# Two scan inputs in one GpSimd instruction, in a fused state-space scan and mixture-of-experts kernel

## The chip, the core and the metric

The kernel runs on one core of a Trainium2 chip. The metric is the device time of one execution in microseconds, lower is better. The core's engines work in parallel, each through its own queue in order, and wait for one another through semaphores. In the profile's names PE is TensorE, DVE is VectorE, ACT is ScalarE, POOL is GpSimd and SP is SyncE, which here issues all transfers.

## The reference, cut to what matters

The input is x of 4 x 1024 tokens by 512 channels. Each batch row passes a modulated layer norm, a depthwise convolution over time that gives `u`, and a selective scan with 16 states per channel:

```python
delta = softplus(einsum('blr,dr->bld', dt, dtproj_w) + dtproj_b)
deltaA = exp(delta[..., None] * A)                       # A: 512 x 16
deltaBu = delta[..., None] * Bm[:, :, None, :] * u[..., None]
h = dA * h + dBu                                         # one step in time
y = einsum('bdn,bn->bd', h, c)
```

Then `x = x + ga * (y + u * D_skip)`, a second modulated norm, and a layer of 8 experts, of which the best two are weighted per token: an up projection to 2048, silu, and a down projection to 512. Weights are float32.

## The kernel before, in words

**Tiles.** The 4096 tokens are 8 chunks of `CT` = 512. In a chunk the scan runs over channel tiles of 128 channels (`r`, 4 of them) and states (`n`, 16 of them), so a chunk has 64 *slots*, numbered `slot(c, n, r)`: r runs fastest. A slot is four steps on four engines:

- ACT, task `da` (line 1065): exp(DEL * AN) into one of two PSUM banks, `DA`.
- POOL, task `dbu` (line 837): `DB = DU * BR`, 128x512, where `DU` is delta*u of the channel tile and `BR` is the row of B of state n, spread over the 128 partitions by a DMA (line 644) into one of two buffers. `DB` has `NDB` = 4 slots.
- DVE, task `scan` (line 1297): the recurrence over 512 tokens, from `DA` and `DB` into `H`. From the second chunk of a batch row on it starts from the stored state `ST`, so its form in the profile is `H<-pb,ST,DB` in odd chunks (counted from 0) and `H<-pb,DB` in even ones.
- PE, task `flip` (line 1563), six slots later: four transposes of H into a work bank; then DVE, task `acc` (line 1322), adds C times that bank to `ACC`.

The last chunk (7) is `SPLIT`: its tokens go in two halves, and `dbu` and `scan` have forms of their own (lines 840 and 1302).

**Beside the scans** of a chunk run the attention preparation of the next chunk and the experts of the chunk before (two halves `cs` of 256 tokens). On POOL these are: `cva` (line 784), part of the convolution; `del` and `du` (lines 795, 801), which make DEL and DU of the next chunk late in this one; `g` (line 860), the product that the down projection takes; `sel1` and `sel2` (lines 557 to 569), the expert weights; `hl` (line 808) and `fin` (line 865). DVE has the `conv` taps (line 1256, with two SBUF inputs and a per-partition weight) and `ys` (line 1371), the factor of g that comes from the up projection. ACT has `th` (line 1167), the tanh, which may overwrite a buffer that g of two blocks before has read, and `ud` (line 1052), which waits for `du`. PE has `up` (lines 1612 to 1614) and `dn` (line 1642).

**The order** is one hand-tuned list of tasks (`schedule`, from tables of places in half slots such as `ATTENTION`, `PAIRS` and `ROUTER`), and every engine runs its own tasks of that list in that order. At slot s the list holds scan s, the flip of slot s - 6, da of slot s + 1, dbu of slot s + 2, then the tasks placed at 2s, the accumulations of the flips of slot s - 1, and the tasks placed at 2s + 1. Every fourth slot it holds the DMA of the row of B two states on; that one waits until the dbu of the state two before it are done. The wait of dbu i for its DB slot is for scan i - 4:

```python
                    if i >= NDB:
                        eng.wait_ge(S["scan"], i - NDB + 1)
```

A semaphore that counts scans is at i - 3 when scans 0 to i - 4 are done.

Of the kernel before, what the change touches and what calls it, by code (L numbers as in the profile page):

```python
# [6 lines left out]
CT, FT = 512, 256  # L7
# [4 lines left out]
NDA, NDB, NG = 2, 4, 3  # L12
# [310 lines left out]
def adaln_kernel(nc, x, pvec, alog, ct, wmod, xpT, dtT, wg1T, wg2T, wupT, bup, wdT, bdn, out):  # L323
# [4 lines left out]
    with ctx:  # L328
# [113 lines left out]
        S = {}  # L442
# [271 lines left out]
        def _(eng):  # L714
            for task in order:
# [32 lines left out]
                elif what == "bdz":  # L748
                    eng.wait_ge(S["modp"], rows_done(2))
                    eng.memset(BDX, 0.0).then_inc(S["bdz"], 1)  # L750
                elif what == "gbk":
                    gate, sign = GBC[:, 0], GBC[:, 1]
                    eng.wait_ge(S["gbm"], 1)
                    eng.tensor_scalar(sign, gate, 0.0, 2.0, ALU.is_ge, ALU.mult).then_inc(S["gbclamp"], 1)
                    eng.wait_ge(S["gbclamp"], 1)
                    eng.tensor_scalar(sign, sign, -1.0, 1.0, ALU.add, ALU.mult).then_inc(S["gbclamp"], 1)
                    eng.wait_ge(S["gbclamp"], 2)
                    eng.tensor_tensor(gate, gate, sign, ALU.mult).then_inc(S["gbclamp"], 1)
                    eng.wait_ge(S["gbclamp"], 3)
                    eng.tensor_scalar(gate, gate, 0.25, 1.0, ALU.max, ALU.mult).then_inc(S["gbclamp"], 1)  # L760
                    eng.wait_ge(S["gbclamp"], 4)
                    eng.tensor_tensor(gate, gate, sign, ALU.mult).then_inc(S["gbclamp"], 1)
                elif what == "nma":
                    eng.wait_ge(S["asm"], 4 * k[0])
                    eng.tensor_scalar(ANG[:], ASM[:], -1.0 / D, 1.0, ALU.mult, ALU.mult).then_inc(S["ang"], 1)
                elif what == "nmf":
                    eng.wait_ge(S["fsm"], 2 * (k[0] + 1))
                    eng.tensor_scalar(FNG[:], FSM[:], -1.0 / D, 1.0, ALU.mult, ALU.mult).then_inc(S["fng"], 1)
                elif what == "pad":
                    c = k[0]  # L770
                    if c == 1:
                        eng.wait_ge(S["modp"], rows_done(4))
                    if c >= 2:
                        eng.wait_ge(S["da"], slot(c - 2, NS - 1, 3) + 1)
                    if c % 2:
                        eng.wait_ge(S["hc"], c // 2 + 1)
                        eng.tensor_copy(hm_of(c)[:, :, 0:3], HC[:]).then_inc(S["pad"], 1)
                    else:
                        eng.memset(hm_of(c)[:, :, 0:3], 0.0).then_inc(S["pad"], 1)
                elif what == "cva":  # L780
                    c, dt, tap = k
                    tap_done(eng, c, dt, tap + 1)
                    eng.wait_ge(S["cvs"], nth["cvs", c, dt, tap])
                    eng.tensor_tensor(U[:, dt], U[:, dt], xn_of(c)[:, 2 + nth[task] % 2], ALU.add).then_inc(S["cva"], 1)
                elif what == "hc" and k[0] % 2 == 0:
                    c = k[0]
                    eng.wait_ge(S["hm"], nth["hm", c, 3])
                    if c > 1:
                        eng.wait_ge(S["pad"], c)
                    eng.tensor_copy(HC[:], hm_of(c)[:, :, 512:515]).then_inc(S["hc"], 1)  # L790
                elif what == "del" and k[0]:
                    c, dt = k
                    eng.wait_ge(S["m"], nth["m", c, dt])
                    eng.wait_ge(S["ln"], 4 * c + dt + 1)
                    eng.tensor_tensor(DEL[:, c % 2, dt], DEL[:, c % 2, dt], xn_of(c)[:, dt], ALU.add).then_inc(
                        S["del"], 1)
                elif what == "du" and k[0]:
                    c, dt = k
                    eng.wait_ge(S["ug"], nth["ug", c, dt])
                    eng.wait_ge(S["del"], nth["del", c, dt])  # L800
                    eng.tensor_tensor(DU[:, c % 2, dt], DEL[:, c % 2, dt], U[:, dt], ALU.mult).then_inc(S["du"], 1)
                elif what == "hl":
                    cs, i = k
                    d = slice(2 * i, 2 * i + 2)
                    if cs >= 2:
                        eng.wait_ge(S["up"], (cs - 1) * NM)
                    eng.wait_ge(S["hh"], cs + 1)
                    eng.tensor_tensor(HLV[cs % 2][:, d], H2F[:, d], HHV[cs % 2][:, d].bitcast(f32),
                                      ALU.subtract).then_inc(S["hl"], 1)
                elif what == "wlo":  # L810
                    i, half = k
                    kk, h = divmod(i, 2)
                    sl = slice(h * 1024 + half * 512, h * 1024 + half * 512 + 512)
                    eng.wait_ge(S["whi"], i + 1)
                    taps = [nth[t] for t in order[:at[task]] if t[0] == "conv"]
                    if taps and taps[-1] > 12:
                        eng.wait_ge(S["conv"], taps[-1])
                    eng.tensor_tensor(WUL[:, kk, sl], WS[h][:, half * 512:half * 512 + 512], WUH[:, kk, sl].bitcast(f32),
                                      ALU.subtract).then_inc(S["wlo"], 1)
                elif what == "r4":  # L820
                    cs = k[0]
                    eng.wait_ge(S["rt"], 6 * cs + 4)
                    eng.tensor_copy(IXF[:], IX[:]).then_inc(S["ixf"], 1)
                elif what in ("sel1", "sel2") and k[0] < NF - 2:
                    select(eng, what, k[0])
                elif what == "dbu":
                    c, n, r = k
                    i = slot(c, n, r)
                    _, h, qs, _, _ = part(c, n, r)
                    if n == 0:  # L830
                        eng.wait_ge(S["du"], nth["du", c, qs[-1]])
                    if r == 0:
                        eng.wait_ge(S[f"d_br{n % 2}"], rows_of_b(c, n))
                    if i >= NDB:
                        eng.wait_ge(S["scan"], i - NDB + 1)
                    if h is None:
                        eng.tensor_tensor(DB[:, i % NDB], DU[:, c % 2, r], BR[:, n % 2], ALU.mult).then_inc(S["dbu"], 1)  # L837
                    else:
                        b = BR[:, n % 2, r // 2 * FT:r // 2 * FT + FT]
                        eng.tensor_tensor(DB[:, i % NDB].rearrange("p (k t) -> p k t", k=2),  # L840
                                          DU[:, c % 2, qs[0]:qs[0] + 2, h * FT:h * FT + FT],
                                          b.unsqueeze(1).to_broadcast([128, 2, FT]), ALU.mult).then_inc(S["dbu"], 1)
                elif what == "frs":
                    cs = k[0]
                    eng.wait_ge(S["fsq"], 2 * (cs + 1))
                    eng.tensor_scalar(FRS[:, :, 0], FSQ[:], 1.0 / D, EPS, ALU.mult, ALU.add).then_inc(S["frs"], 1)
                    eng.wait_ge(S["frs"], 3 * cs + 1)
                    eng.tensor_tensor(FRS[:, :, 0], FRS[:, :, 0], MH[:, 0:2], ALU.pow).then_inc(S["frs"], 1)
                    eng.wait_ge(S["frs"], 3 * cs + 2)
                    eng.tensor_tensor(FNM[:, :, 0], FNG[:], FRS[:, :, 0], ALU.mult).then_inc(S["frs"], 1)  # L850
                elif what == "g":
                    cs, m = k
                    i = cs * NM + m
                    eng.wait_ge(S["ys"], i + 1)
                    eng.wait_ge(S["t1"], i + 1)
                    if i >= NG and in_parts((i - NG) // 2):
                        eng.wait_ge(S["gl"], nth["gl", *divmod(i - NG, NM)])
                    elif i >= NG:
                        eng.wait_ge(S["dn1"], i - NG + 1)
                    eng.tensor_tensor(G[:, i % NG], TH[:, m % 2], YS[:, m % 2], ALU.mult).then_inc(S["g"], 1)  # L860
                elif what == "fin":
                    cs, j = k
                    acc = acc_tile(cs // 2, 2 * (cs % 2) + j)
                    eng.wait_ge(S["to"], nth["to", cs, j])
                    eng.tensor_tensor(acc, acc, TO[:, j], ALU.add).then_inc(S["fin"], 1)
# [818 lines left out]
```

## Time and profile before

| what | value |
|---|---|
| three runs | 1390.89, 1391.97, 1392.40 us |
| median | 1391.97 us |
| the profiled execution, first to last instruction | 1389.7 us |
| PE busy | 1310.4 us (94%) |
| DVE busy | 1228.5 us (88%) |
| POOL busy | 1136.4 us (82%) |
| ACT busy | 988.3 us (71%) |
| TensorE clock granted, mean | 0.977 of full speed |

The profile gives the profiled execution's span, 1389.7 us; its own device time is not given apart, and the span lies 2.3 us under the median of the runs. In a row of instructions, `L837 POOL TENSOR_TENSOR DB<-DU,BR ... x448 | 576.6, 1304 | 43.6 <-DVE H L1297 36.7` reads: line 837, on POOL, 448 of them, busy 576.6 us together, 1304 ns each on the mean; POOL was idle for 43.6 us just before them, and of that 36.7 us ended with a scan of line 1297.

### The profile page before, as it was taken

The page shows a single profiled execution, that of the slowest core. Times are in us where ns is not written, and L with a number is a line of the kernel's source. Part 1 is how long each engine was busy: PE and PEld are TensorE (multiplying, and loading weights), DVE is VectorE, ACT ScalarE, POOL GpSimd, SP SyncE. Part 2 cuts the span into 40 slices and gives each one's busy share as a digit, 9 for nine tenths or more (in the row PEclk, how much of TensorE's full clock was granted, in tenths as well). Part 3 has the DMA queues.
Part 4 walks back from the last instruction along what each step waited for, and adds up shares of the span by engine and source line. Part 5 has one row for each costly group of instructions (what it writes and reads, how often), then busy time and mean ns, then how long its engine had stood idle before and what let it go on. Part 6 is the DMA issues. An engine that isn't in the chain of part 4 may idle for free. (4 is left out here: it accounts for less than half of the span.)

```text
span 1389.7 us, 23827 instructions
## 1 busy us (share of the span) xinstructions
PE 1310.4 (94%) x7664; PEld 977.8 (70%) x7664; DVE 1228.5 (88%) x1729; ACT 988.3 (71%) x2110; POOL 1136.4 (82%) x1177
## 2 busy tenths in 40 slices
PE   8888768999999999999999999999999999989998
PEld 4466546767776777777776777767776776768897
DVE  4899999989998999989998999999998999885565
ACT  4875786588857786588858786688758775745654
POOL 1799889799997999799998999799988987762332
PEclk9999867999999999999999999999999999999999
DMA  5542112325342424434342434334253423323342
GB/s 201 177 154 62 61 39 90 115 78 170 94 148 86 161 97 123 132 111 156 90 144 85 164 97 125 125 113 146 87 148 100 129 85 116 108 74 125 112 125 79
DMA packets 99284, 160.94 MB, mean 116 GB/s; under 512 B 9276, under 2 KB 33980, under 8 KB 99160
## 3 DMA queue, kind: packets, MB, share of 16 engines
q1 hardware_dynamic: 99160, 159.42, 36.3%
q8 instruction: 61, 1.00, 0.3%
q14 instruction: 63, 0.52, 0.1%
HBM read 150.60 MB, written 8.79 MB: 115 GB/s over the span
## 5 line engine op out<-in xcount | busy, mean ns | idle before, releaser
L837 POOL TENSOR_TENSOR DB<-DU,BR 128x512 f32<-128x512 f32 x448 | 576.6, 1304 | 43.6 <-DVE H L1297 36.7
L1322 DVE SCALAR_TENSOR_TENSOR ACC<-pb,CTM,ACC 128x512 f32<-128x512 f32 x512 | 373.6, 730 | 42.4 <-PE pb L1563 41.5
L1642 PE MATMUL pb<-WD,G 128*128 128x512 f32 x856 | 406.0, 594 | 0.0
L1065 ACT ACTIVATE pb<-DELP,AN 128x512 f32<-128x512 f32 x448 | 305.8, 685 | 107.5 <-DVE H L1297 105.3
L1563 PE MATMUL pb<-ID,H 128*128 128x128 f32 x2048 | 311.9, 280 | 32.9 <-DVE ACC L1322 25.3
L1563 PEld LDWEIGHTS pb<-ID,H 128*128 128x128 f32 x2048 | 244.0, 144 | 137.0 <-issue 77.5
L1612 PE MATMUL pb<-H2H,WUH 128*128 128x256 f32 x1024 | 326.7, 319 | 12.0 <-DVE TY L1371 11.8
L1297 DVE TENSOR_TENSOR_SCAN H<-pb,DB 128x512 f32<-128x512 f32 x256 | 309.7, 1211 | 13.4 <-ACT pb L1065 12.3
L1614 PE MATMUL pb<-H2H,WUL 128*128 128x256 f32 x1024 | 290.5, 284 | 0.0
L1613 PE MATMUL pb<-H2L,WUH 128*128 128x256 f32 x1024 | 290.2, 283 | 0.0
L860 POOL TENSOR_TENSOR G<-TY 128x256 f32<-128x256 f32 x256 | 188.9, 756 | 99.7 <-ACT TY L1172 44.3
L1297 DVE TENSOR_TENSOR_SCAN H<-pb,ST,DB 128x512 f32<-128x512 f32 x192 | 244.1, 1271 | 7.3 <-ACT pb L1065 7.3
L1642 PEld LDWEIGHTS pb<-WD,G 128*128 128x128 f32 x856 | 149.3, 191 | 108.7 <-issue 107.5
L1612 PEld LDWEIGHTS pb<-H2H,WUH 128*128 128x128 f32 x1024 | 196.3, 192 | 36.2 <-issue 26.4
L1167 ACT ACTIVATE TY<-pb,BUPH 128x256 f32<-128x256 f32 x256 | 108.8, 469 | 149.5 <-PE pb L1614 137.2
L1613 PEld LDWEIGHTS pb<-H2L,WUH 128*128 128x128 f32 x1024 | 196.9, 192 | 13.3 <-issue 12.7
L1614 PEld LDWEIGHTS pb<-H2H,WUL 128*128 128x128 f32 x1024 | 196.2, 192 | 0.0
L1371 DVE SCALAR_TENSOR_TENSOR TY<-pb,BUP,SR 128x256 f32<-128x256 f32 x256 | 110.5, 472 | 35.7 <-ACT TY L1167 32.8
L1172 ACT ACTIVATE TY<-TY 128x256 f32<-128x256 f32 x256 | 102.1, 412 | 0.0
L1302 DVE TENSOR_TENSOR_SCAN H<-pb,ST,DB 128x256 f32<-128x256 f32 x128 | 88.4, 732 | 6.4 <-ACT pb L1070 4.3
L840 POOL TENSOR_TENSOR DB<-DU,BR 128x512 f32<-128x512 f32 x64 | 81.2, 1281 | 4.1 <-DVE H L1302 4.1
L1256 DVE SCALAR_TENSOR_TENSOR U<-DELP,PV,U 128x512 f32<-128x512 f32 x57 | 59.6, 1059 | 0.8
(220 smaller groups left out, 1700.0 us busy)
## 6 DMA issues: line engine op xcount, KB each, us to landing
WD<-in_wdT SPq DMA_DIRECT2D x128, 512.0 KB, 4.7
BR<-bscr SPq DMA_DIRECT2D x112, 256.0 KB, 3.7
SR<-sscr SPq DMA_DIRECT2D x128, 128.0 KB, 4.6
ACC<-in_x SPq DMA_DIRECT2D x16, 512.0 KB, 4.0
out<-ACC SPq DMA_DIRECT2D x32, 256.0 KB, 3.0
DU<-in_x SPq DMA_DIRECT2D x7, 1024.0 KB, 5.6
BR<-bscr SPq DMA_DIRECT2D x32, 128.0 KB, 3.1
DU<-in_xpT SPq DMA_DIRECT2D x7, 320.0 KB, 3.1
```

Of the source, the lines that this page charges most:

```text
L837: eng.tensor_tensor(DB[:, i % NDB], DU[:, c % 2, r], BR[:, n % 2], ALU.mult).then_inc(S["dbu"], 1)
L860: eng.tensor_tensor(G[:, i % NG], TH[:, m % 2], YS[:, m % 2], ALU.mult).then_inc(S["g"], 1)
L1065: eng.activation(DA[i % NDA][:], DEL[:, c % 2, r], ACT.Exp, scale=AN[:, r, n:n + 1]).then_inc(S["da"], 1)
L1167: eng.activation(TH[:, m % 2], up_of(cs, m), ACT.Tanh, scale=0.5, bias=BUPH[:, m:m + 1]).then_inc(S["th"], 1)
L1297: eng.tensor_tensor_scan(H[:, (c * NS + n) % NH, r], DA[i % NDA][:], DB[:, i % NDB], ST[:, n, r:r + 1] if state_from(c, h) else 0.0, ALU.mult,
L1322: eng.scalar_tensor_tensor(out=acc, in0=banks[bank_of["flip", c, n, r]][:], scalar=1.0 if n < 0 else CTM[:, c % 2, j, st:st + 1], in1=acc, ...
L1371: eng.scalar_tensor_tensor(out=YS[:, m % 2], in0=up_of(cs, m), scalar=BUP[:, m:m + 1], in1=SR[:, m // 2 % 2], op0=ALU.add, op1=ALU.mult).t ...
L1563: t = eng.transpose(b[:, dt * 128:dt * 128 + 128], src[:, dt, r * 128:r * 128 + 128], ID[:])
L1612: eng.matmul(b, WUH[:, kk, sl], H2H[:, cs % 2, kk], start=kk == 0, stop=False)
L1613: eng.matmul(b, WUH[:, kk, sl], H2L[:, cs % 2, kk], start=False, stop=False)
L1614: t = eng.matmul(b, WUL[:, kk, sl], H2H[:, cs % 2, kk], start=False, stop=kk == 3)
L1642: eng.matmul(DN[j][:], G[:, (cs * NM + m) % NG, j * 128:j * 128 + 128], WD[:, (cs * NE + m // 2) % NWD, m % 2], start=False, stop=m == NM ...
```

## The change

For the chunks that aren't split, the dbu of two neighbouring channel tiles (r and r + 1, r even) become one instruction over 128x1024. It stands where the first of the two stood in the list; where the second stood there is nothing. It writes two neighbouring slots of DB, and reads two tiles of DU and the one row of BR twice, by an address step of zero. It waits for one more scan (i - 3 in place of i - 4) and, in state 0, for the du of the second tile; its end raises the count by 2, so scans, transfers and all that counts dbu keep their numbers. State 0 of chunk 0 and all of chunk 7 keep the old instructions.

```diff
                     _, h, qs, _, _ = part(c, n, r)
+                    both = h is None and (c, n) != (0, 0)
+                    if both and r % 2 == 1:
+                        continue
                     if n == 0:
-                        eng.wait_ge(S["du"], nth["du", c, qs[-1]])
+                        eng.wait_ge(S["du"], nth["du", c, r + 1 if both else qs[-1]])
                     if r == 0:
                         eng.wait_ge(S[f"d_br{n % 2}"], rows_of_b(c, n))
+                    if both:
+                        if i >= NDB:
+                            eng.wait_ge(S["scan"], i - NDB + 2)
+                        eng.tensor_tensor(DB[:, i % NDB:i % NDB + 2], DU[:, c % 2, r:r + 2],
+                                          BR[:, n % 2:n % 2 + 1].to_broadcast([128, 2, CT]), ALU.mult).then_inc(S["dbu"], 2)
+                        continue
                     if i >= NDB:
                         eng.wait_ge(S["scan"], i - NDB + 1)
```

## Rows read from the trace of the kernel before

**Rows 1.** The page: busy time by engine, and in 40 slices
```profile
PE 1310.4 (94%) x7664; PEld 977.8 (70%) x7664; DVE 1228.5 (88%) x1729; ACT 988.3 (71%) x2110; POOL 1136.4 (82%) x1177
DVE  4899999989998999989998999999998999885565
```

**Rows 2.** Windows: start:end, length, then PE, PEld, DVE, ACT, POOL busy us
```profile
130.00:140.00 10.00, 7.18 (x49) 5.91 (x50) 10.00 (x13) 7.47 (x16) 7.69 (x7) 1.00 0.25 83
...
400.00:450.00 50.00, 49.43 (x283) 35.45 (x282) 44.61 (x64) 35.47 (x78) 40.97 (x43) 1.00 0.37 112
450.00:500.00 50.00, 48.75 (x296) 37.08 (x296) 47.82 (x62) 41.97 (x94) 48.35 (x52) 1.00 0.46 150
```

**Rows 3.** Groups by line: busy us, mean ns, idle before them, its releasers
```profile
L837 POOL TENSOR_TENSOR DB<-DU,BR 128x512 f32<-128x512 f32 x448 | 576.6, 1304 | 43.6 <-DVE H L1297 36.7 <-DVE DU L1279 6.1 <-DMA BR<-bscr 0.6
L860 POOL TENSOR_TENSOR G<-TY 128x256 f32<-128x256 f32 x256 | 188.9, 756 | 99.7 <-ACT TY L1172 44.3 <-DVE TY L1371 42.2 <-PE pb L1642 8.7
L840 POOL TENSOR_TENSOR DB<-DU,BR 128x512 f32<-128x512 f32 x64 | 81.2, 1281 | 4.1 <-DVE H L1302 4.1
L1256 DVE SCALAR_TENSOR_TENSOR U<-DELP,PV,U 128x512 f32<-128x512 f32 x57 | 59.6, 1059 | 0.8
```

**Rows 4.** Who waited for whom, all of the trace: us, times, longest
```profile
DVE ACC L1322 <- PE pb L1563: 41.5, 62, 1.9
ACT U L1052 <- POOL DU L801: 14.4, 8, 2.1
ACT TY L1167 <- POOL G L860: 11.7, 20, 1.6
```

**Rows 5.** Line 837 by itself: who waited for it
```profile
  DVE H L1297: 0.6, 2
```

**Rows 6.** POOL in order of time: start, us (a run's together), line, count
```profile
403.20 1.28 POOL L837 TENSOR_TENSOR DB<-DU,BR 128x512 f32<-128x512 f32 x1 [0.27 <-DVE H L1297]
404.43 1.41 POOL L860 TENSOR_TENSOR G<-TY 128x256 f32<-128x256 f32 x2
...
441.64 0.71 POOL L562 TENSOR_SCALAR S<-IO,IXF,RS 128x104 f32<-128x104 f32 x1
...
462.42 3.74 POOL L837 TENSOR_TENSOR DB<-DU,BR 128x512 f32<-128x512 f32 x3
466.11 2.53 POOL L801 TENSOR_TENSOR DU<-DELP,U 128x512 f32<-128x512 f32 x2
468.60 1.45 POOL L860 TENSOR_TENSOR G<-TY 128x256 f32<-128x256 f32 x2
470.00 2.51 POOL L837 TENSOR_TENSOR DB<-DU,BR 128x512 f32<-128x512 f32 x2
```

**Rows 7.** DVE in order of time, the same columns
```profile
404.47 1.21 DVE L1297 TENSOR_TENSOR_SCAN H<-pb,DB 128x512 f32<-128x512 f32 x1
...
414.19 0.75 DVE L1322 SCALAR_TENSOR_TENSOR ACC<-pb,CTM,ACC 128x512 f32<-128x512 f32 x1 [1.42 <-PE pb L1563]
...
436.37 1.21 DVE L1297 TENSOR_TENSOR_SCAN H<-pb,DB 128x512 f32<-128x512 f32 x1
...
450.42 1.21 DVE L1297 TENSOR_TENSOR_SCAN H<-pb,DB 128x512 f32<-128x512 f32 x1
...
471.49 1.28 DVE L1297 TENSOR_TENSOR_SCAN H<-pb,ST,DB 128x512 f32<-128x512 f32 x1
```

**Rows 8.** PE in order of time: the down products of the g at 404.43
```profile
410.34 1.88 PE L1642 MATMUL pb<-WD,G 128*128 128x512 f32 x4
```

**Rows 9.** A convolution tap on DVE, and POOL around it
```profile
385.12 1.87 DVE L1256 SCALAR_TENSOR_TENSOR U<-DELP,PV,U 128x512 f32<-128x512 f32 x1
...
383.92 2.52 POOL L784 TENSOR_TENSOR U<-U,DU 128x512 f32<-128x512 f32 x2
386.40 1.74 POOL L837 TENSOR_TENSOR DB<-DU,BR 128x512 f32<-128x512 f32 x1
```

**Rows 10.** Line 1256 by itself: shortest, median and longest ns
```profile
L1256 DVE SCALAR_TENSOR_TENSOR U<-DELP,PV,U x57: 737/829/2928, 17.5 to 1010.7; 128x512 f32<-128x512 f32 x57
```

## The prediction

> **What bounds the kernel now.** I read the engines' busy time first. PE has 94%, DVE 88%, POOL 82%, and in the slices DVE stands at 8 and 9 tenths nearly everywhere but in the last fifth, where the split chunk and the tail run and nothing is changed [rows 1]. The stretches by window tell them apart. Until about 240 us DVE is the full engine: 10.00 of 10 us at 130, with PE at 7.18. From 300 to 1085 us PE is the fullest, 49.43 and 48.75 of 50 us, with DVE at 44.61 and 47.82 and POOL at 40.97 and 48.35; the second of these windows holds the border between two chunks, the first the middle of one [rows 2]. Then I asked who waits for whom. DVE waits 41.5 us for transposes on PE [rows 4], and waited for a DB of POOL in two places only, 0.6 us together [rows 5]. POOL itself stood idle for 36.7 us before dbu because the scan that frees the slot had not ended, and 99.7 us before g [rows 3]. So POOL is busy but it is nobody's bound: DB is ready early, and what ACT waits for it (14.4 and 11.7 us, [rows 4]) is mostly taken up by ACT's own idle time.
>
> **Part 1, the instruction.** 448 products of 512 become 444 of them in 222 pairs, plus the four of chunk 0, state 0. What one costs POOL is read from starts, not from durations, since neighbours overlap by some 40 ns: three that take 3.74 us have 466.11 - 462.42 = 3.69 between their first start and the next task's, so 1.23 each; two g of half the size take 470.00 - 468.60 = 1.40, so 0.70 each [rows 6]. The slope is (1.23 - 0.70)/256 = 2.07 ns an element, and a pair comes to 1.23 + 512 x 0.00207 = 2.29; I take 2.31. That is 0.16 less than two, 222 x 0.16 = 35 us of POOL's 1136. The mean durations (756 and 1304, [rows 3]) would give 2.40 against 2.61, the same kind of saving. The address step of zero costs nothing by the nearest row: the split form repeats its row of BR in that way and takes 1281 against 1304 [rows 3]. Bounds: no saving at all, 2 x 1.23 = 2.46, and with a penalty that no row shows, 2.6; below, 2.2.
>
> From the Trainium skill, GPSIMD Engine Reference, section on performance against the Vector engine, comes another point: a two-input add over 2048 elements takes 4497 ns. An estimate between that page's figure and 1.23 at 512 would be 2.32 for a pair, within 0.01 of what I take, and no sum below needs it.
>
> The 35 us leave an engine that nobody waits for. Directly on the path they are worth the 0.6 us of the two waits.
>
> **Part 2, the later wait and the coarser grain.** The first DB of a pair is ready 2.31 - 1.23 = 1.08 us later after the start than alone, and the start waits for one scan more. In mid chunk this is covered: POOL idles there on the scans anyway (36.7 us, [rows 3]), and a pair that starts when scan i - 3 ends has scans i - 2 and i - 1 ahead of it. Two scans of 1.21 and two accumulations of at most 0.75 [rows 7], their overlaps off, take about 3.6 us, against 2.31. The tasks behind the pair on POOL pay. The g at 404.43 stands behind the dbu at 403.20; as a pair that one waits for the scan at 404.47 to end, 405.68, so 2.5 us more, and it is longer by 1.1, together 3.6 us [rows 6, 7]. The g ended at 405.84, and its down products started at 410.34 [rows 6, 8]. The 4.5 us of cover is enough. SP isn't held either: the row of B waits for a count that is reached no later than before.
>
> The tight place is the chunk border, where del, du, g and fin of the next chunk crowd on POOL without a gap. The scan at 471.49 is the first of chunk 3 (its form changes there to one with ST), so by counting back 15 scans the one at 436.37 is scan 49 [rows 7]. I follow POOL from there. The pair for slots 52 and 53 starts when scan 49 ends, 437.6, and ends at 439.9; the two sel of 0.70 each bring POOL to 441.3 in place of 441.64, 0.3 early [rows 6]. From there to 470.00 lie ten dbu, so five pairs, 0.8 earlier; but the pair for 58 and 59 must wait for scan 55 (450.42 + 1.21 = 451.6, [rows 7]), which gives 0.5 to 0.6 back. The pair for the first two slots of chunk 3 thus starts about 0.5 early, at 469.5, and ends at 471.8, where the scan wants it at 471.49: 0.35 us late, in place of 0.2 early. The later pairs catch up. The same pattern, with the same tasks, stands at six borders, the even ones with 0.2 more room: 6 x 0.3 = 1.8 us. About half of it is made good behind it, because DVE then waits less for PE (1.42 us before the accumulation at 414.19 is such a wait, [rows 7]). I count **+0.9 us**, between 0 and 11: at 2.48 a pair the five pairs of the burst bring nothing and each border loses 1.1 us and more in the next pairs, which comes to 6 x 1.8 = 11.
>
> **Part 3, DVE's taps against a longer instruction.** The row of the taps shows a block, not a slowdown. The shortest takes 737 ns, the longest 2928 [rows 10]. The one at 385.12 takes 1.87 us: POOL's two additions run until 386.44, and the tap ends 0.55 us after them; the dbu that starts at 386.40 takes 1.74 in place of 1.27, so it stood still until the tap was through [rows 9]. The Trainium skill, SBUF — State Buffer, practical consequences, has this as a rule: a DVE instruction with two SBUF inputs and a GpSimd instruction that reads SBUF exclude each other for a whole instruction, and the one that started first goes first. By that rule, which these rows bear out, a longer instruction speaks against this change. The price from rows: the 57 taps spend 59.6 - 57 x 0.74 = 17.4 us on such waits. dbu holds 576.6/1136.4 = 51% of POOL's busy time, and for a tap that meets one the rest of it grows by 2.31/1.23 = 1.88; the waits become 17.4 x (1 + 0.51 x 0.88) = 25.2, +7.8 us at most. Which tap meets which instruction is chance, for each starts anew by the shifted order; below, the change could even gain a few us. The taps run from 17.5 to 1010.7 us [rows 10], and only in the first quarter of that, up to 240, is DVE the full engine and each wait counts; of the rest, DVE's waits for PE take up the most. I count a quarter of 7.8, **+2.0 us**, between -3 and +7.8.
>
> **Sum.** -0.6 + 0.9 + 2.0 = +2.3 us. Against the profiled execution that is a span of 1389.7 + 2.3 = 1392.0; with the 2.3 us by which the median lies above that span, the time is **1394.3 us**.
>
> **Rivals.**
> - *The border becomes a stall of DVE* (slower). Place: the first two pairs of each chunk. It decides as soon as a pair costs POOL more than about 2.4 us. Price at 2.48: 11 us, so 1391.97 + 11 = 1403; at 2.6 it would be 5 us a border. For it: POOL has 48.35 of 50 us there and the first DB had 0.2 us of room. Against it: the slope of the two sizes. Chance 0.13.
> - *The block by longer instructions* (slower). The full 7.8 us on the path: 1399.8. For it: the 1.87 and 2928 ns rows. Against it: PE, not DVE, is the fullest from 300 us on. Chance 0.15.
> - *POOL was the brake after all* (faster). The burst ends 0.5 us earlier at each border, ACT's eight waits for du shrink by as much, 8 x 0.45 = 3.6, with the 0.6: 1391.97 - 4.2 = 1387.8. For it: 26.1 us of ACT's waits for POOL. Against it: DVE, which takes ACT's results, waits for POOL 0.6 us. Chance 0.12.
> - *The instruction isn't one*: the chip works through the two rows as dearly as through two instructions, and the places even out: 1392 to 1394. Chance 0.05; the rest of that case is the first rival.
>
> **How the numbers follow.** The forecast itself has 0.55, and its own spread of some 3 us lies around 1394.3. A measurement of this kernel can tell about 0.2%, 2.8 us, from no change, so 1389.2 to 1394.8 is the same. Of the 0.55, 0.35 lie within, 0.14 above, 0.06 below. With the rivals: slower 0.14 + 0.13 + 0.15 = 0.42; faster 0.06 + 0.12, less some of that rival that stays inside the 0.2%, 0.17; the same 0.41. The range goes from the faster rival, 1387.5, to the first slower one, 1403.
>
> **What the profile would show.** Line with DB: 222 instructions of 128x1024 with starts 2.3 apart, POOL's busy time near 1100 us. Right: DVE's waits for a DB of a few us in all, at the six borders, none in mid chunk; taps of line 1256 with a mean of 1.1 to 1.2 us and one or more above 1.9; POOL's idle time on scans well above 36.7 us. Wrong: a pair above 2.4 us, waits of DVE for DB above 10 us, g starting so late that PE or ACT name it, or a time off by more than 3 us with none of these.

## The result and the profile after

The changed kernel takes 1411.86 us (median of 4 runs, 1410.36 to 1413.54) against 1392.16 for the kernel before (4 runs). The ratio is 1.0145 with a 95% interval of 1.0131 to 1.016: slower by about 20 us, where I had forecast +2.3 us and a range that ended at 1403. The profiled execution has a span of 1411.8 us, so 22.1 us more than before.

The page of the kernel after, busy time by engine and the same slices:

```profile
PE 1316.5 (93%) x7664; PEld 984.1 (70%) x7664; DVE 1232.1 (87%) x1729; ACT 990.3 (70%) x2110; POOL 1105.8 (78%) x955
DVE  4899899889898999989898999989998999886565
```

Groups by line of the kernel after (from the changed place on, lines lie nine further down than before: 837 is 846, 860 is 869, 1297 is 1306, 1563 is 1572; columns as in [rows 3]):

```profile
L840 POOL TENSOR_TENSOR DB<-DU,BR 128x1024 f32<-128x1024 f32 x222 | 529.6, 2388 | 89.8 <-DVE H L1306 88.2 <-issue 1.1
L1265 DVE SCALAR_TENSOR_TENSOR U<-DELP,PV,U 128x512 f32<-128x512 f32 x57 | 60.0, 1065 | 0.9
L1608 PE MATMUL pb<-ID,S 128*104 128x128 f32 x32 | 6.7, 293 | 12.9 <-POOL S L569 10.3 <-DVE S L569 2.6
```

POOL is busy for 30.6 us less. DVE and PE have the same instructions as before and are busy for 3.6 and 6.1 us longer. Of the 6.1, 3.1 fall before chunk 1, where the mean granted clock of PE is 0.92 in place of 0.95. In chunk 1 it is 0.86 in both traces and in chunks 2 to 6 it is 1.00 in both, so the clock isn't what takes the time there. What grew are waits. Who waited for POOL, in the kernel before and then in the one after (us, times, longest):

```profile
ACT TY L1167 <- POOL G L860: 11.7, 20, 1.6
PE pb L1599 <- POOL S L569: 2.7, 1, 2.7
ACT DU L976 <- POOL U L784: 2.2, 2, 1.6
```

```profile
POOL DB L840 <- DVE H L1306: 88.2, 73, 3.0
ACT TY L1176 <- POOL G L869: 20.1, 26, 2.2
PE pb L1608 <- POOL S L569: 10.3, 6, 4.9
ACT DU L985 <- POOL U L784: 9.5, 6, 1.9
DVE H L1306 <- POOL DB L840: 6.6, 4, 2.0
```

PE now waits 10.3 us for the expert weights (line 569, task `sel2`), and ACT 9.5 us for the additions of the convolution (line 784, task `cva`). Neither is in the ring of DB at all.

**Where the time was lost.** Every scan can be found in both traces, so the start of the same scan tells how far the changed kernel is behind. I took the differences of that lag over stretches of slots. (The profiled execution is the slowest of the four, so the table adds up to 22.1 us and not to the 19.7 between the medians.)

| stretch | lag gained, us |
|---|---|
| up to chunk 1 | 1.1 |
| chunk 1 | 8.5 |
| chunks 2 to 6, slots 0 to 19, sum of five | -1.2 |
| slots 19 to 32 | 9.1 |
| slots 32 to 60 | 0.1 |
| slots 60 to 64, the border | 3.3 |
| chunk 7 and the tail | 1.2 |

The loss isn't spread. In chunks 2 to 6 it falls where slots 19 to 32 lie and at the border, and of the 8.5 us of chunk 1, 6.4 fall between its slots 20 and 40. In slots 32 to 60 the pairs wait for scans most (48.0 of their 61.9 us in chunks 2 to 6), and nothing is lost.

**Slots 20 to 24 of chunk 3**, POOL in order of time, first before, then after (the same places of the list; 11.1 us of lag stood between them at slot 20):

```profile
511.09 1.28 POOL L837 TENSOR_TENSOR DB<-DU,BR 128x512 f32<-128x512 f32 x1
512.31 2.54 POOL L808 TENSOR_TENSOR H2L<-XT,H2H 128x512 fp32r<-128x512 f32 x2
514.81 2.54 POOL L837 TENSOR_TENSOR DB<-DU,BR 128x512 f32<-128x512 f32 x2
517.29 0.20 POOL L823 CAST IXF<-IX 128x16 f32<-128x16 uint32 x1
517.67 1.44 POOL L557 TENSOR_SCALAR S<-IO,IXF,RS 128x104 f32<-128x104 f32 x2 [0.17 <-issue]
...
521.92 0.23 POOL L569 TENSOR_TENSOR S<-S,SHI 128x16 f32<-128x16 f32 x1
522.11 1.30 POOL L837 TENSOR_TENSOR DB<-DU,BR 128x512 f32<-128x512 f32 x1
...
526.45 1.28 POOL L784 TENSOR_TENSOR U<-U,DU 128x512 f32<-128x512 f32 x1
```

```profile
523.59 2.38 POOL L840 TENSOR_TENSOR DB<-DU,BR 128x1024 f32<-128x1024 f32 x1 [1.30 <-DVE H L1306]
525.93 2.54 POOL L808 TENSOR_TENSOR H2L<-XT,H2H 128x512 fp32r<-128x512 f32 x2
528.42 2.38 POOL L840 TENSOR_TENSOR DB<-DU,BR 128x1024 f32<-128x1024 f32 x1
530.73 0.20 POOL L823 CAST IXF<-IX 128x16 f32<-128x16 uint32 x1
...
535.62 0.22 POOL L569 TENSOR_TENSOR S<-S,SHI 128x16 f32<-128x16 f32 x1
...
537.72 2.37 POOL L840 TENSOR_TENSOR DB<-DU,BR 128x1024 f32<-128x1024 f32 x1
540.05 2.65 POOL L784 TENSOR_TENSOR U<-U,DU 128x512 f32<-128x512 f32 x2
```

Before, the weights begin (line 823) at 517.29. With the lag that would be 528.4; they begin at 530.73, 2.3 us late. The delay comes from the pair for slots 20 and 21. Before, the product for slot 20 began at 511.09, which would be 522.2 with the lag. The pair waits 1.30 us for scan 17 and begins at 523.59, and it takes 1.1 us longer than that product alone, so `hl` behind it is 2.5 us late. The next pair, at 528.42, starts as soon as `hl` is through (scan 19, for which it waits, had ended at 527.42), and passes the delay on. The first `cva` comes at 540.05 instead of 526.45 + 11.1 = 537.6. PE and ACT of the kernel after, the instructions that needed these:

```profile
535.89 0.43 PE L1608 MATMUL pb<-ID,S 128*104 128x128 f32 x2 [1.12 <-POOL S L569]
```

```profile
541.41 0.72 ACT L985 ACTIVATE DU<-DELP,PV 128x512 f32<-128x512 f32 x1 [1.84 <-POOL U L784]
542.04 0.40 ACT L1181 ACTIVATE TY<-TY 128x256 f32<-128x256 f32 x1
542.35 1.29 ACT L1074 ACTIVATE pb<-DELP,AN 128x512 f32<-128x512 f32 x2
```

And DVE, behind both of them:

```profile
538.29 0.75 DVE L1331 SCALAR_TENSOR_TENSOR ACC<-pb,CTM,ACC 128x512 f32<-128x512 f32 x1 [0.62 <-PE pb L1572]
...
543.15 1.28 DVE L1306 TENSOR_TENSOR_SCAN H<-pb,ST,DB 128x512 f32<-128x512 f32 x1 [1.50 <-ACT pb L1074]
```

ACT stood idle for 1.84 us before a scaling for the convolution whose buffer the late `cva` still reads; the exponential for the next scan is queued behind it, and the scan starts 1.50 us late. This is a wait of DVE for ACT by the profile's words, and of ACT for POOL by its cause. At the border the same kind of chain runs through `g`: ACT's tanh waits for it, and DVE's `ys` for the tanh (columns as above, ACT and then DVE; both at the end of chunk 2):

```profile
473.28 0.47 ACT L1176 ACTIVATE TY<-pb,BUPH 128x256 f32<-128x256 f32 x1 [2.12 <-POOL G L869]
```

```profile
474.54 0.88 DVE L1380 SCALAR_TENSOR_TENSOR TY<-pb,BUP,SR 128x256 f32<-128x256 f32 x2 [0.56 <-ACT TY L1176]
```

### The profile page after: what moved, and what is told of

The parts are those of the page before. It is cut to its first block and busy times, and to the rows that moved or that the text cites. A ratio compares the mean times of both kernels' runs of the same rounds, so it can differ in the third digit from the quotient of the medians.

```text
span 1411.8 us, 23704 instructions
## 1 busy us (share of the span) xinstructions
PE 1316.5 (93%) x7664; PEld 984.1 (70%) x7664; DVE 1232.1 (87%) x1729; ACT 990.3 (70%) x2110; POOL 1105.8 (78%) x955
## 5 line engine op out<-in xcount | busy, mean ns | idle before, releaser
L840 POOL TENSOR_TENSOR DB<-DU,BR 128x1024 f32<-128x1024 f32 x222 | 529.6, 2388 | 89.8 <-DVE H L1306 88.2
L1331 DVE SCALAR_TENSOR_TENSOR ACC<-pb,CTM,ACC 128x512 f32<-128x512 f32 x512 | 374.0, 731 | 49.1 <-PE pb L1572 47.4
L869 POOL TENSOR_TENSOR G<-TY 128x256 f32<-128x256 f32 x256 | 193.8, 775 | 99.4 <-ACT TY L1181 46.7
L849 POOL TENSOR_TENSOR DB<-DU,BR 128x512 f32<-128x512 f32 x64 | 81.1, 1280 | 4.2 <-DVE H L1311 4.2
L1453 PE MATMUL pb<-H2H 128*128 128x256 f32 x292 | 58.7, 335 | 3.1 <-ACT H2H L896 3.1
```

Source lines behind the costliest of these rows:

```text
L840: eng.tensor_tensor(DB[:, i % NDB:i % NDB + 2], DU[:, c % 2, r:r + 2], BR[:, n % 2:n % 2 + 1].to_broadcast([128, 2, CT]), ALU.mult).then_i ...
L1331: eng.scalar_tensor_tensor(out=acc, in0=banks[bank_of["flip", c, n, r]][:], scalar=1.0 if n < 0 else CTM[:, c % 2, j, st:st + 1], in1=acc, ...
```

## The experiments

The theories held against each other: **A**, the order of the work. What stands behind the pair on POOL comes late, because the pair waits for one scan more (A1) or because it brings the second product forward (A2). **B**, the length of one instruction, with the time in which it shuts out DVE's two-input instructions. Each expectation was written before its run; "the change" in them is the changed kernel. The kernel before ran beside each on the same chip.

### e1: two products at the pair's place

```diff
-                        if i >= NDB:
-                            eng.wait_ge(S["scan"], i - NDB + 2)
-                        eng.tensor_tensor(DB[:, i % NDB:i % NDB + 2], ...).then_inc(S["dbu"], 2)
+                        for j in (0, 1):
+                            if i + j >= NDB:
+                                eng.wait_ge(S["scan"], i + j - NDB + 1)
+                            eng.tensor_tensor(DB[:, (i + j) % NDB], DU[:, c % 2, r + j], BR[:, n % 2],
+                                              ALU.mult).then_inc(S["dbu"], 1)
```

> The two products stand where the pair stands, but as two instructions of 128x512, the second alone with the later wait. Theory A (order: what stands behind the pair on GpSimd waits for a later scan and for a second product, and the expert weights, the cva and some g come late): the loss stays, 1409 to 1416 us, and PE still waits about 10 us for the weights of line 569. Theory B (length: a DB is ready only when the whole 1024 are, and a DVE tap is shut out for longer): the loss goes, 1392 to 1396 us. Theory C (the pair costs GpSimd more than two products): 1392 to 1396 as well.

Measured: 1397.2 us against 1391.4, ratio 1.0044 (1.0027 to 1.006). A, as I had written it, missed: most of the loss went, and PE waits 6.5 us for line 569, not about 10. The 1392 to 1396 of B (and of C, a pair that costs POOL more than two products, which the 2.31 us below rule out) was nearer and missed too, by 1.2 us. This run changes two things at once, for the first product also got its early wait back. It took e5 to part them.

### e2 and e3: six slots of DB

```diff
-NDA, NDB, NG = 2, 4, 3
+NDA, NDB, NG = 2, 6, 3
...
-        JUNK = sb("JUNK", [128, 3, D])
+        JUNK = sb("JUNK", [128, 3, D], mybir.dt.bfloat16)
```

(and `ABS` laid into `ST` to make room.) e2 has the pairs, e3 the single products.

> The pairs with six slots of DB in place of four, so that a pair waits for scan i - 5 in place of i - 3 (room comes from a scratch of ScalarE in bf16 and one reused tile). Theory A1 (of the order it is the later wait that counts): 1390 to 1398 us and GpSimd's idle time on scans falls from 88 us to under 30. Theory A2 (it is the second product's 1.1 us ahead of the others): 1402 to 1410 us. Theory B (length): 1408 to 1414 us, unchanged.

> Control: the kernel before with the same six slots, bf16 scratch and reused tile. All theories: within 3 us of the kernel before, 1389 to 1395 us, as DVE waited for a DB for 0.6 us only. If it is faster by more, a longer ring is worth something by itself and e2 is to be held against this run.

Measured: e2 1410.9 us against 1391.4, 1.0141 (1.0124 to 1.0157); e3 1392.2, 1.0007 (0.9997 to 1.0016). The waits for scans went, as wanted, and the time did not come back. It was the result B had forecast (A2's range ended 0.9 us below it), though e1 had just spoken for something else. The rows of e2 say why; groups by line:

```profile
L841 POOL TENSOR_TENSOR DB<-DU,BR 128x1024 f32<-128x1024 f32 x222 | 530.5, 2399 | 7.3 <-DVE H L1307 6.2 <-issue 1.0
L1358 DVE TENSOR_TENSOR RS<-RS 128x2 f32<-128x2 f32 x16 | 10.8, 677 | 0.1
L1266 DVE SCALAR_TENSOR_TENSOR U<-DELP,PV,U 128x512 f32<-128x512 f32 x57 | 66.3, 1175 | 0.6
```

POOL's idle time on scans is 6.2 us in place of 88.2. But the taps take 66.3 us, 6.7 more than [rows 3], and a product of two numbers per partition that takes 394 ns on the mean in the kernel before takes 677. DVE and POOL of e2 around it:

```profile
521.05 1.49 DVE L1358 TENSOR_TENSOR RS<-RS 128x2 f32<-128x2 f32 x1
...
528.80 2.79 DVE L1266 SCALAR_TENSOR_TENSOR U<-DELP,PV,U 128x512 f32<-128x512 f32 x1
```

```profile
520.15 2.37 POOL L841 TENSOR_TENSOR DB<-DU,BR 128x1024 f32<-128x1024 f32 x1
...
528.66 2.39 POOL L841 TENSOR_TENSOR DB<-DU,BR 128x1024 f32<-128x1024 f32 x1
```

Both stand still until the pair is through. The product of two numbers, whose shortest takes 0.14 us, ends at 522.54, and the pair at 520.15 + 2.37 = 522.52. The tap, whose shortest takes 0.72 us, ends at 531.59, and the pair at 528.66 + 2.39 = 531.05. In the whole trace of e2, 13 taps and 5 of these products begin inside a pair; every one of the taps ends 0.55 us after its pair, and every one of the products 0.02. That is the rule of the Trainium skill, SBUF — State Buffer, practical consequences, and these rows agree with it. A POOL that no longer waits for scans met these instructions at other moments, and here at worse ones.

### e4 and e8: pairs in some places only

```diff
-                    both = h is None and (c, n) != (0, 0)
+                    both = h is None and (c, n) != (0, 0) and (c == 0 or n not in (5, 6))
```

for e4, and for e8 `and c > 1 and n not in (0, 5, 6, 14, 15)`.

> The change, but states 5 and 6 (slots 20 to 27) of chunks 1 to 6 keep single products. Theory A (the loss of slots 20 to 28, some 1.6 to 2.2 us a chunk and 4 to 5 in chunk 1, comes from the weights and cva behind the pairs there): 1396 to 1402 us. Theory B (length, spread over all pairs): a sixth of 20 us back at most, 1408 to 1411 us.

> Pairs in chunks 2 to 6 only, and there not in states 0, 5, 6, 14 and 15 (110 pairs left of 222), that is in places where the traces show no slot lost. Theory A (single places): 1390 to 1394 us, no loss. Theory B (length everywhere): half the loss, 1399 to 1403 us.

Measured: e4 1397.9 us, 1.0047 (1.003 to 1.0064); e8 1394.9, 1.0027 (1.0017 to 1.0038). In e4, 24 of the 222 pairs went and 13 of the 20 us came back: the places decide, not the number. (It doesn't tell A from B, since the taps lie in these places too.) e8 missed its 1390 to 1394 by a little; its lag grows at slot 4 of the chunks (0.99 us in chunk 3, where the scan waits 0.91 us for its DB), a place that I had taken for harmless because the full change loses nothing there.

### e5: both products behind the late wait

```diff
+                        if i >= NDB:
+                            eng.wait_ge(S["scan"], i - NDB + 2)
                         for j in (0, 1):
-                            if i + j >= NDB:
-                                eng.wait_ge(S["scan"], i + j - NDB + 1)
                             eng.tensor_tensor(DB[:, (i + j) % NDB], ...).then_inc(S["dbu"], 1)
```

> Two products of 128x512 at the pair's place, and both behind the pair's later wait. Against e1 (1397.2) only the first product's wait changes; against the change (1411.9) only the length. Theory A (the wait for scan i - 3 ahead of the first product delays what stands behind): 1407 to 1413 us, with the weights of line 569 as late for PE as in the change. Theory B (length, with its lock against DVE's two-input instructions): 1396 to 1399 us. If it lies between, the two shares can be read off.

Measured: 1410.7 us, 1.0147 (1.013 to 1.0164), which is what A forecast, and as far above its kernel before (19.6 us) as the change (19.7). PE waits 15.4 us for line 569:

```profile
PE pb L1609 <- POOL S L569: 15.4, 6, 4.8
```

With four slots, the pair as one instruction makes no difference that can be told (the intervals of the two figures reach some 2 us to each side); the loss is there without it.

### e6: one instruction at the place of the second product

The pair is issued at r odd, over slots i - 1 and i, with the wait for scan i - 4 that the second product has (i is the second slot here).

> One instruction of 128x1024, but at the place where the second product stood, so that weights, cva and g between the two places go first. Theory A: most of the loss goes, 1393 to 1400 us, with somewhat more waits of DVE for a DB (10 us or so). Theory B (length): the loss stays, 1408 to 1414 us.

Measured: 1429.9 us, 1.028 (1.0263 to 1.0298). Both theories missed, A by 30 us. Line 1265 of e6, the taps, and who waited for line 840:

```profile
L1265 DVE SCALAR_TENSOR_TENSOR U<-DELP,PV,U x57: 730/1066/2914, 17.3 to 1045.2; 128x512 f32<-128x512 f32 x57
```

```profile
  DVE H L1306: 13.0, 11
```

The taps' median went from 829 [rows 10] to 1066 ns, and their sum to 74.2 us, 14.6 more; DVE waits 13.0 us for a DB. The scan lags by 30.5 us over chunks 2 to 6, 13.6 of it in slots 32 to 60, where the change loses 0.1. The tasks between the two places go first, but the first DB of each pair now comes too late. How the 38.8 us divide between the late DB and the taps was not tried apart.

### e7 and e11: the weights one half slot earlier

```diff
-             "r31": 37, "e1": 36, "r4": 40, "r41": 37, "r42": 39, "sel1": 40, "sel2": 40, "r5": 41, "r52": 42,
+             "r31": 37, "e1": 36, "r4": 39, "r41": 37, "r42": 39, "sel1": 39, "sel2": 39, "r5": 41, "r52": 42,
```

e7 is this on the change, e11 on the kernel before.

> The change, with the expert weights of the even halves (r4, sel1, sel2) one half slot earlier, so that they stand ahead of the pair for slots 22 and 23 and not behind it. Theory A: PE's wait for line 569 falls from 10 us to under 3 and the loss at slots 21 to 23 goes; as the cva stand behind the same work as before, the delay of ACT at slot 24 stays in part: 1402 to 1409 us. Theory B: no difference, 1409 to 1414 us.

> The kernel before with the even halves' expert weights one half slot earlier, as in e7. PE waits for line 569 only some 3 us in the kernel before, most of it in chunk 1. A gain of 0 to 2 us, 1389.5 to 1392 us; if the tiny product on DVE meets GpSimd more often, 0 to 2 us slower.

Measured: e7 1408.2 us, 1.0124 (1.0107 to 1.0141); e11 1390.4, 0.9996 (0.9987 to 1.0006), no difference. In e7 PE's wait for line 569 is 1.9 us in place of 10.3, as forecast, and of the 19.7 us above the kernel before beside it 17.1 are left. So moving the weights gave back 2.6 us, hardly more than the intervals. ACT's wait for `cva` stays (11.4 us in all), here at slot 24 of chunk 3, and so does the scan's:

```profile
538.35 0.73 ACT L985 ACTIVATE DU<-DELP,PV 128x512 f32<-128x512 f32 x1 [1.70 <-POOL U L784]
```

```profile
540.09 1.28 DVE L1306 TENSOR_TENSOR_SCAN H<-pb,ST,DB 128x512 f32<-128x512 f32 x1 [1.42 <-ACT pb L1074]
```

### e9 and e10: the two missing corners

```diff
-                        eng.wait_ge(S["scan"], i - NDB + 1)
+                        eng.wait_ge(S["scan"], i - NDB + 1 + (h is None and (c, n) != (0, 0) and r % 2 == 0))
```

is e9, on the kernel before. e10 is e2 with the two products of e1 in place of the pair.

> The kernel before, every product in its own place and of 128x512, with one thing changed: the first of each two waits for scan i - 3 in place of i - 4. With e1 (together, early wait, 1397.2) and e5 (together, late wait, 1410.7) this fills the square. If the wait costs by itself what it costs together (13.5 us), 1403 to 1406 us; if it only costs when the second product stands behind it too (a burst of 2.5 us ahead of weights and cva), 1392 to 1398 us. Length plays no part here.

> Six slots of DB and two products of 128x512 at the pair's place, no late wait. Against e2 (one instruction, 1410.9) only the length changes. If the loss of e2 is the lock (a two-input instruction of DVE shut out for 2.4 us: 0.95 us at slot 20, 1.1 at slot 22, 1.2 to 1.6 at slot 27 of each chunk), 1394 to 1400 us, with the tiny product of expert weights on DVE back from 677 to about 400 ns and the taps from 1175 to under 1050 ns. If the loss is the order alone, 1408 to 1412 us.

Measured: e9 1398.4 us, 1.0052 (1.0035 to 1.0069), 0.4 us above the 1392 to 1398 that I had written for a wait that costs little by itself. e10 1397.1, 1.0046 (1.003 to 1.0063), in the range of the lock; taps 945 ns and the tiny product 427 ns on the mean. Groups by line of e10:

```profile
L842 POOL TENSOR_TENSOR DB<-DU,BR 128x512 f32<-128x512 f32 x444 | 563.9, 1295 | 3.3 <-DVE H L1308 2.4 <-DMA BR<-bscr 0.7
L1267 DVE SCALAR_TENSOR_TENSOR U<-DELP,PV,U 128x512 f32<-128x512 f32 x57 | 53.1, 945 | 0.8
```

**Where e2 loses more than e10.** By the same lags, e2 loses 10.5 us more than e10 in slots 19 to 32 of chunks 2 to 6, 4.7 more in slots 32 to 60, and 1.1 less at the borders. The first part lies where the blocked instructions are: in chunk 3 the tiny product at 521.05 and the tap at 528.80 take 1.49 and 2.79 us, and 0.54 and 1.20 in e10. The second part has another link. In e2, PE stands idle around slot 22 and its granted clock then falls to the lower level, 1.2 GHz, for 3.4 us; first the idle time (a line of PE in order of time), then the clock (a window as in [rows 2]; the 0.50 is the granted clock, as a share of full speed):

```profile
376.16 0.66 PE L1582 MATMUL pb<-ID,XT 128*128 128x128 f32 x4 [2.04 <-DVE ACC L1332]
```

```profile
377.00:380.40 3.40, 3.40 (x8) 1.67 (x7) 3.40 (x5) 2.50 (x6) 3.10 (x3) 0.50 0.06 21
```

All five chunks from 2 to 6 have such a stretch in e2; the kernel before, the change, e1 and e10 have none there and lose 0.1 us or less in slots 32 to 60. e5 tells what it costs. PE stands idle for 2.12 us there in each of the five chunks, and the clock falls in chunks 4, 5 and 6 and not in 2 and 3: e5 loses 0.64, 0.71 and 0.63 us in slots 32 to 60 of the former, and 0.00 in the latter. In e2 it is 0.91 to 0.98 us a chunk. The loss arrives as a longer wait of DVE for the transposes; e5 in chunks 3 and 5, at the same place of the list:

```profile
575.41 0.75 DVE L1332 SCALAR_TENSOR_TENSOR ACC<-pb,CTM,ACC 128x512 f32<-128x512 f32 x1 [0.88 <-PE pb L1573]
```

```profile
888.96 0.75 DVE L1332 SCALAR_TENSOR_TENSOR ACC<-pb,CTM,ACC 128x512 f32<-128x512 f32 x1 [1.59 <-PE pb L1573]
```

**What follows.** Each number is a median less that of the kernel before on the same chip, in us, with an interval of some 2 us to each side; the products are of 128x512 but where the row says one instruction. The kernel before with six slots (e3) is 0.7 us above the one with four.

| products | slots of DB | wait of the first | us |
|---|---|---|---|
| each in its place | 4 | scan i - 3 (e9) | +7.3 |
| together | 4 | scan i - 4 (e1) | +5.8 |
| together | 4 | scan i - 3 (e5) | +19.6 |
| one instruction | 4 | scan i - 3 (the change) | +19.7 |
| together | 6 | scan i - 6 (e10) | +6.1 |
| one instruction | 6 | scan i - 5 (e2) | +19.5 |

The later wait alone costs 7.3, the place alone 5.8, and both together 19.6, so 6.5 more than their sum. The two lose in different places. In chunks 2 to 6 the wait alone (e9) loses 4.6 us in slots 19 to 32 and 0.1 at the border, the place alone (e1) nothing in slots 19 to 32 and 3.5 at the border; both together (e5) lose 7.0 and 4.1. With four slots the length adds nothing that can be told. With six, where POOL hardly waits for scans (2.4 us in e10, 6.2 in e2), the length costs 19.5 - 6.1 = 13.4 us. In that pair of runs the first product also waits for one scan more; with 3.8 us of such waits between them I take that to be small, but no run has it alone. So the change couldn't win by a larger ring: the loss by the wait is then replaced by the loss by the length, which is the blocked instructions of DVE and the 4.7 us that come behind PE's lower clock. None of the versions is measurably faster than the kernel before.

## Why the prediction was wrong

- **What bounds the kernel: right, and read too far.** DVE and PE bound it, and POOL's own busy time doesn't matter: 30.6 us less of it (35 forecast) bought nothing. The step "POOL is busy but it is nobody's bound" then made me look only at the DB. PE already waited 2.7 us for `sel` and ACT 2.2 us for `cva` in the kernel before. Those small rows, quoted above, are the ones that grew most for their size, to 10.3 and 9.5 us.
- **Part 1: right.** The pair lasts 2388 ns and its starts to the next task are 2.31 (528.42 to 530.73) to 2.33 apart (537.72 to 540.05), against 2.31. The step of zero costs nothing. (By these terms the saving is 2.46 - 2.31 = 0.15 us a pair, 33 us, and not the 0.16 and 35 that I wrote.)
- **Part 2: this step failed.** "The tasks behind the pair on POOL pay" was right; the term was +0.9 us, and the place with its wait measures 19.6 (e5). I followed one `g` with 4.5 us of cover, and walked the border for the DB, 0.35 us late. The weights and the `cva` at slots 20 to 24, which had less cover, weren't followed at all. That these two and `g` carry the loss is read from the traces: of the 19.7 us, e7 gave back 2.6 by moving the weights, and no run moved the `cva` or the `g` alone. At the border the DB was not what came late: DVE's scan at 482.66 had its DB from 480.07 + 2.38 = 482.45. A `g` before it came late, and cost 0.56 us of DVE through the tanh, so the border has about twice the forecast loss (3.3 us for five) by another chain. DVE's 6.6 us of waits for DB are four, three of 1.97 us at places where it waited 1.97 for ACT before, so they are hardly new.
- **Part 3: right in mechanism, wrong in place.** The taps take 60.0 us against 59.6, where I had counted +2.0. The block is real and the length costs 13.4 us as soon as POOL doesn't wait for the scans (e2 against e10). With four slots the taps grow too by the length, from 49.7 us in e5 to 60.0 in the change, while PE's wait for line 569 shrinks from 15.4 to 10.3. That these two cancel is argued, not shown, and a third thing differs: the stretches at the lower clock, which e5 has in three chunks and the change in none.
- **The made-good half.** I let DVE's waits for PE take up what it loses. They didn't: PE was late too, behind the weights, and DVE's wait for transposes rose from 41.5 [rows 4] to 47.4 us.
- **The rivals.** The first had the sign and about half the size (11 us), but its mechanism, a pair above 2.4 us and DB late at the border, isn't what happened. The second has a real mechanism, but the taps' sum rose by 0.4 us and not by 7.8. POOL was no brake that could be eased: with 30.6 us less work on it the time rose. Of my signs of being wrong, one came true: PE names `g` (1.4 us), which it never did before, and ACT for 20.1 us in place of 11.7.

What stays open: chunk 1 loses 8.5 us with the pairs and 4.1 in e5, and which of its waits make up the difference was not tried. Part of it may be the spread between executions: the profiled one of e5 was the fastest of its four (1408.2 us) and that of the change the slowest of its four (1413.5), while their medians are equally far from the kernel before. PE waits 4.93 us for line 569 there, the longest of all.

## What to carry to other kernels

On an engine that runs its queue in order, ask of every task behind the changed one how long its result lies idle before it is read, and start with the waits that are small but already there: here they marked results without room. A second piece of work pulled forward and a wait pulled forward cost more together here than apart (19.6 us against 7.3 and 5.8); both delay the same tasks, and my explanation is that each alone still fits in part into the cover that these tasks have. Merging two GpSimd instructions saved 0.14 us a pair here, of an engine that must be the bound to profit, and lengthens what DVE's two-input instructions may have to wait for.

## What the runs showed of the hardware that was not expected

A DVE instruction over 128x2 took 1.49 us in e2, where the shortest of its line takes 0.14, because it has two SBUF inputs and met a GpSimd instruction of 2.37 us. It lost more than nine times its own length, and its line, with 10.8 us in all, stands far down in a list by busy time. The wait is inside the instruction's own duration and not in the idle time before it, so it is found by the shortest and the longest of a line. That a GpSimd held up by waits for scans meets DVE's two-input instructions less badly than one that runs free I had not expected either: taps of 49.7 us in e5 against 53.1 in e10, and of 60.0 in the change against 66.3 in e2. It is no rule, for e6, held up for 83.6 us, has taps of 74.2.

An idle time of PE of 2 us around slot 22 was followed by 3.4 us at 1.2 GHz in some places and not in others, not even in each chunk of one run (e5: three of five), and each such stretch came with a loss of 0.6 to 1.0 us in slots 32 to 60 of its chunk.
